# Graph network layer: VectorE instead of TensorE adds the gathered rows to z, and 26 instead of 28 quads are done by counts

## The reference

```python
h = jnp.maximum(_layernorm(x, axis=-1), 0.0)
e = jnp.concatenate([h[src], h[dst]], axis=1)          # 200000 x 128
m = jax.nn.relu(e @ W1 + b1) @ W2 + b2                 # W1 128x128, W2 128x64
s = jax.ops.segment_sum(m, dst, num_segments=12500)
cnt = jax.ops.segment_sum(ones, dst, num_segments=12500)
x = x + s / jnp.maximum(cnt, 1.0)[:, None]
```

## Time and profile before

| | us |
|---|---|
| runs | 2848.26, 2846.46, 2843.46; median 2846.46 |
| the profiled execution, whole | 2839.25 |
| its span | 2837.4 |
| TensorE matmul busy | 1548.3 (55%) |
| VectorE busy | 1428.9 (50%) |
| ScalarE busy | 1189.8 (42%) |
| GpSimd busy | 1372.7 (48%) |
| TensorE clock granted, mean | 0.749 of full |
| DMA, mean | 144 GB/s |

### The profile page before, as it was taken

How to read it: one execution, slowest core, us unless ns; L and a number is a source line. 1 busy time by engine, 2 the same in 40 slices (tenths; PEclk the granted TensorE clock), 3 DMA queues, 4 the chain that set the end, 5 groups by cost and what they waited for, 6 DMA issues and landing times.

```text
span 2837.4 us, 26976 instructions
## 1 busy us (share of the span) xinstructions
PE 1548.3 (55%) x8249; PEld 1183.2 (42%) x8250; DVE 1428.9 (50%) x3051; ACT 1189.8 (42%) x2414; POOL 1372.7 (48%) x1460
## 2 busy tenths in 40 slices
PE   1656565566465564455544555455455545555556
PEld 0545353444344443344433444344344434434444
DVE  3554343343324665456655666456565556655421
ACT  1223343444314544345444454344344444444444
POOL 6345545445555445444554435545544554554553
PEclk6878777788787777677776777767776777776778
DMA  4532222222134656556565566556565665665541
GB/s 90 163 109 60 59 61 59 60 59 58 58 98 144 202 181 189 167 169 200 179 192 154 178 188 200 186 159 183 184 192 168 186 191 174 183 186 157 174 119 43
DMA packets 258990, 408.46 MB, mean 144 GB/s; under 512 B 45128, under 2 KB 118749, under 8 KB 258841
## 3 DMA queue, kind: packets, MB, share of 16 engines
q1 hardware_dynamic: 211845, 312.84, 35.7%
q0 software_dynamic: 46432, 93.61, 12.5%
q10 hardware_dynamic: 564, 0.23, 0.0%
HBM read 388.12 MB, written 18.38 MB: 143 GB/s over the span
## 4 chain that ended last, share of the span: by engine, by line
PE 48%; issue 36%; another core or an unknown queue 9%; DVE 6%; ACT 1%; DMA 0%; DVEq 0%; SPq 0%; ACTq 0%
PE z L1374 16%; PE bank L1401 12%; PE z L1386 10%; DVE g L1153 4%; PE bank L1419 2%; PE bank L1408 2%; PE z L1445 2%; PE bank L1430 1%; PE z L1461 1%; DVE rows_b L936 1%; PE bank L1268 1%; DVE norms L920 1%; PE z L1268 1%; ACT g L812 0%
## 5 line engine op out<-in xcount | busy, mean ns | idle before, releaser
L672 POOL DMA_INDIRECT g<-p_table,src_e x1403 | 1326.1, 945 | 1425.3 <-PE bank L1401 960.5
L1153 DVE SCALAR_TENSOR_TENSOR g<-z,norms,g 128x1024 bf16<-128x1024 f32 (+1 forms) x884 | 1019.1, 1214 | 43.5 <-issue 25.3
L812 ACT ACTIVATE g<-z 128x1024 f32<-128x1024 f32 x182 | 185.6, 1020 | 1468.0 <-remote 1153.5
L1100 DVE TENSOR_TENSOR acc<-acc,bank 65x128 f32 x191 | 54.2, 284 | 1201.0 <-remote 1069.7
L1374 PE MATMUL z<-work 128*128 128x128 f32 x1464 | 258.8, 348 | 514.2 <-issue 482.9
L1374 PE MATMUL z<-w,work 128*128 128x128 f32 x1438 | 251.9, 345 | 484.3 <-issue 443.8
L1374 PEld LDWEIGHTS z<-work 128*128 128x128 f32 x1464 | 240.3, 256 | 546.0 <-issue 541.7
L1374 PEld LDWEIGHTS z<-w,work 128*128 128x128 f32 x1438 | 234.4, 253 | 512.3 <-issue 509.3
L1401 PE MATMUL bank<-work,g 128*128 128x128 f32 x2902 | 423.4, 307 | 15.4 <-issue 15.1
L1401 PEld LDWEIGHTS bank<-work,g 128*128 128x128 f32 x2902 | 414.1, 227 | 16.8 <-issue 16.7
L1386 PE MATMUL z<-g,ident 128*128 128x512 f32 x726 | 350.8, 605 | 5.8 <-issue 5.7
(11 more groups left out here) (161 smaller groups left out, 1063.6 us busy)
## 6 DMA issues: line engine op xcount, KB each, us to landing
g<-tally_table SPq DMA_DIRECT2D x816, 256.0 KB
rel_q<-rel_table SPq DMA_DIRECT2D x46, 512.0 KB
rows_b<-rel_table SPq DMA_DIRECT2D x45, 512.0 KB
g<-p_table,src_e POOLq DMA_INDIRECT x1403
g<-tally_table SPq DMA_DIRECT2D x68, 128.0 KB
work<-q_table SPq DMA_DIRECT2D x96, 64.0 KB
w<-q_table SPq DMA_DIRECT2D x96, 64.0 KB
g<-p_table SPq DMA_DIRECT2D x12, 512.0 KB
```

The costliest lines, as they stand in the source:

```text
L672: nc.gpsimd.indirect_dma_start(out=g[:, slot(n), j * HID:(j + 1) * HID], out_offset=None, in_=p_table, in_offset=bass.IndirectOffsetOnAxis ...
L812: nc.scalar.activation(rows_of_p(m), z[:, 0:HID * chunks_in(m)], ACT.Relu).then_inc(r_done, 1)
L1153: nc.vector.scalar_tensor_tensor(product[i % BUFFERS][:, 0:w], turned[:, 0:w], minus_q[:, d:d + 1], tally_row[i % BUFFERS][:, 0:w], ALU.ma ...
```

## The change

- `add_rows(m)` moves from TensorE to VectorE. One `tensor_tensor` adds z (PSUM) and the gathered rows (SBUF, `g`), and writes the sum over the gathered rows. It comes after the members and the tally rows of round m, and before `dense(m)` with its products.
- `relu` reads and writes these rows in `g`, no longer PSUM.
- `spread_q(m+1)` waits for VectorE's add of couple m (`z_done`) instead of the relu of couple m.
- TensorE's order becomes: `times_w2` of couple m-2, `sum_edges(m-1)`, `spread_q(m+1)`, `dense(m)`; so a couple's sum comes one round later. The waits that VectorE's own order now covers are dropped.
- 26 quads by counts: DENSE falls from 68 to 59, tallies from 236 to 212 (five a round, rounds 3 to 45, all low one-hot rows on ScalarE), products from 884 to 767 (rounds 52 to 176), and there are 183 couples.

```diff
-Q0 = 28
-GROUP_SIZES = ((128, 4), (320, 2), (QT * 128, 1))
+Q0 = 26
+GROUP_SIZES = ((126, 4), (320, 2), (QT * 128, 1))
-ROUND_TALLIES, TALLY_ROUND, TALLY_PLACES = 6, 3, 12
-VECTOR_TALLIES = (1, 4)
+ROUND_TALLIES, TALLY_ROUND, TALLY_PLACES = 5, 3, 10
-SPAN_ROUNDS = [10] * (SPANS - 1) + [6]
+SPAN_ROUNDS = [10] * (SPANS - 1) + [5]
...
             def relu(m):                                   # ScalarE
                 act.wait_ge(z_done, m + 1)
-                nc.scalar.activation(rows_of_p(m), z[:, 0:HID * chunks_in(m)], ACT.Relu).then_inc(r_done, 1)
+                nc.scalar.activation(rows_of_p(m), rows_of_p(m), ACT.Relu).then_inc(r_done, 1)
...
             def spread_of(m):                              # VectorE
-                if m >= 2:
-                    dve.wait_ge(zq_done, m - 1)
                 dve.wait_ge(rows_there[m // 2 % 2], 16 * (m // 4 + 1))
...
+            def add_rows(m):                               # VectorE
+                dve.wait_ge(zq_done, m + 1)
+                if 2 * m < RAW:
+                    dve.wait_ge(raw_p_done, 2 * m + 2)
+                else:
+                    dve.wait_ge(gathered[slot(Q0 + 2 * m) // 2], rows_landed(m))
+                nc.vector.tensor_tensor(rows_of_p(m), z[:, 0:HID * chunks_in(m)], rows_of_p(m), ALU.add)\
+                    .then_inc(z_done, 1)
...
-                if on_vector(p):
-                    nc.vector.tensor_scalar(low_hot[p % TALLY_PLACES], low_digits, low_key[:, j:j + 1], 0.0,
-                                            ALU.is_equal, ALU.add, accum_out=...)
...
                         for p in tallies(m):               # VectorE, round m
                             high_hot_of(p)
+                        add_rows(m)
                         dense(m)
...
             def spread_q(m):                               # TensorE
                 if m:
-                    pe.wait_ge(r_done, m)
+                    pe.wait_ge(z_done, m)
-                                                qw[i % WINDOWS], start=c == 0, stop=False)
+                                                qw[i % WINDOWS], start=True, stop=True)
-            def add_rows(m):
-                ...
-                    last = nc.tensor.matmul(z[:, 512 * (n % 2):512 * (n % 2) + w], ident[:, :], g[:, slot(n), 0:w],
-                                            start=False, stop=True)
...
-                for m in range(COUPLES):                   # TensorE
-                    add_rows(m)
-                    if m >= 2 and m - 2 == BLOCK_END[BLOCK[m - 2]]:
-                        times_w2(BLOCK[m - 2])
-                    dense(m)
-                    if m + 1 < COUPLES:
-                        spread_q(m + 1)
-                    sum_edges(m)
+                for m in range(COUPLES + 3):
+                    if m - 1 in (COUPLES - 2, COUPLES - 1):
+                        sum_edges(m - 1)
+                    if 2 <= m < COUPLES + 2 and m - 2 == BLOCK_END[BLOCK[m - 2]]:
+                        times_w2(BLOCK[m - 2])
+                    if 1 <= m < COUPLES - 1:
+                        sum_edges(m - 1)
+                    if m + 1 < COUPLES:
+                        spread_q(m + 1)
+                    dense(m)
```

More of the change, by code:

```diff
@@ L170 @@
 MEMBER_FROM = PRODUCT_ROUND
[L173 to L179, removed]
 def products_in(m):
@@ L304, in gnn_kernel @@
         low_hot = [above_ring(512 + 256 * k, 256, BF16) for k in range(TALLY_PLACES)]
-        high_hot = [above_ring(3584 + 64 * k, 64, BF16)[:, 0:125] for k in range(TALLY_PLACES)]
-        tally_stage = above_ring(4352, 256, U16)[0:125, :]
-        q_dense = above_ring(4352, 128, F32)[0:DENSE, :]
+        high_hot = [above_ring(3072 + 64 * k, 64, BF16)[:, 0:125] for k in range(TALLY_PLACES)]
+        tally_stage = above_ring(3712, 256, U16)[0:125, :]
+        q_dense = above_ring(3712, 128, F32)[0:DENSE, :]
         tally_row = [above_ring(512 * k, 512, U16) for k in range(BUFFERS)]
@@ L313, in gnn_kernel @@
         digit_i, digit, src_of_edge = (norms[:, NC * k:NC * (k + 1)] for k in range(3))
[L314 to L318, removed]
+        high_key, low_key = (norms[:, SPANS * DENSE + NC * k:SPANS * DENSE + NC * (k + 1)] for k in range(2))
+        added, by_count = (norms[:, SPANS * DENSE + DENSE * k:SPANS * DENSE + DENSE * (k + 1)] for k in range(2))
+        minus_q = norms[:, 1020:1020 + DENSE]
+        edges_d, of_node = norms[0:125, 1081:1081 + DGROUPS], norms[0:125, 1095:1095 + PER_GROUP]
+        assert 3 * NC <= SPANS * DENSE and SPANS * DENSE + 2 * NC <= 1020 and DENSE <= min(61, NC) and DGROUPS <= 14
         work = sb("work", [128, STAGES * UNIT_COLS + 512])
@@ L782, in spread_of @@
             def spread_of(m):
-                if m == SPREAD_FROM:
-                    act.wait_ge(spread_done, parts_to(m))
                 act.wait_ge(rows_there[m // 2 % 2], 16 * (m // 4 + 1))
@@ L846, in dense @@
                         stage_tallies(i)
-                of = [p for p in tallies(m) if not on_vector(p)]
+                of = tallies(m)
                 for p in of[0:1]:
                     far_low_of(p)
-                for p, after in zip(of, of[1:] + [None]):
-                    if after:
-                        far_low_of(after)
+                for p in of:
+                    if p + 1 in of:
+                        far_low_of(p + 1)
                     low_hot_of(p)
@@ L1126, in edge_keys_of @@
                     .then_inc(edge_keys, 1)
-                nc.vector.scalar_tensor_tensor(low_key, digit, -512.0, src_of_edge, ALU.mult, ALU.add)\
+                nc.vector.scalar_tensor_tensor(low_key, digit, 512.0, src_of_edge, ALU.mult, ALU.subtract)\
                     .then_inc(edge_keys, 1)
@@ L1137, in high_hot_of @@
                 if p == 0:
-                    dve.wait_ge(edge_keys, 10)
+                    dve.wait_ge(edge_keys, 5)
                 if p >= TALLY_PLACES:
@@ L1437, in tally @@
                 pe.wait_ge(high_hot_done, p + 1)
-                if not on_vector(p):
-                    pe.wait_ge(low_hot_done, on_scalar_to(p + 1))
+                pe.wait_ge(low_hot_done, p + 1)
                 if p == TALLY_FIRST[i]:
```

32 lines of the change are left out of this document (7 added, 25 removed).

## The result

| kernel | median, us | lowest to highest | ratio to before, 95% interval |
|---|---|---|---|
| before | 2844.96 | 2843.35 to 2848.26 | |
| changed | 2619.43 | 2612.39 to 2625.56 | 0.9205, 0.918 to 0.9231 |

The changed kernel takes 225 us less. The forecast was 2760 us: the time lies in its range, but the gain is 7.9% where 3.0% was forecast. The profiled execution took 2625.56 us, its span 2623.7.

A forecast was written before the change was run, and what follows sets the result against it. Bound: a loop of waits, 30.67 us for two couples, with TensorE's results withheld to the gather batch's end. 2839.25 - 86 - 14 + 14 = 2753, said as 2760 us; range 2610 to 2900, central forecast 2700 to 2820.

The forecast's parts named there:

- mix of hits and misses: Per gather batch: a hit has the next spread's result in time; a product-stretch miss, only at 22.8 us, loses about 2.0.
- A loop of waits bounds the kernel: GpSimd's batches: results of early matmuls reach others only at 22.8 us, making a loop of 30.67 us for two couples.
- TensorE's add worth nothing: In the loop: dropping TensorE's 1.88 us add a couple gains nothing by itself, since it stands behind the sum releasing GpSimd.
- The order "is what matters": TensorE: with the sum one round behind its spread, relu and spread leave the path behind the late results.
- Hit 28.4 us: Product stretch: only handover, copy, W2, sum and release follow the late result; 28.4 for 30.67, gaining 2.3 us.
- Four hits of five: Product stretch, 60 batches: 0.8 gain 2.3 us and 0.2 lose 2.0, together -86 us.
- rival 1: All product batches hit (-138) and three of four tally batches go at 23.1: 2656 us; chance 0.24 with beyond.
- Tally stretch -14 us: 19 batches at 29.3 us: half hits at 23.1, half misses at 34.0, mean 28.55, so -14 us.
- One couple more, +14: Whole kernel: the added couple costs half a loop, +14 us, its eight more gathers included.
- Sum: Whole kernel: 2839.25 - 86 - 14 + 14 = 2753 us, given as 2760 for a median.
- Clock: TensorE: fewer matmuls could keep its clock down, a batch's first 16 records taking 3.75 instead of 1.95 us; left unpriced separately.
- Rival 4: GpSimd's gathers lose VectorE's 1.22 us an add, +2.4 a batch, +220 over 91 batches: 3066 us; chance 0.03.

The follow-up runs named there:

- gatherless kernels: Kernel before and changed kernel, each with every gather after the first ring of places left out: 1781.4 and 1697.94 us.
- after_batch8: Changed kernel with GpSimd waiting for the sums before every couple (8 gathers), not every second (16): 2318.29 us, 0.8192 to before.
- add28_oldorder: Kernel before with the add on VectorE, TensorE's order as before and 28 quads by counts: 2526.44 us, 0.8925 to before.
- swap: Kernel before with only sum_edges(m) put ahead of spread_q(m + 1), add still on TensorE: 2672.21 us, 0.9448 to before.
- count26: Kernel before with 26 quads by counts alone, add still on TensorE: 2828.11 us, 0.9996 to before.
- before_batch8: Kernel before with GpSimd waiting for the sums before every couple (8 gathers), not every second: 2303.12 us, 0.8134 to before.
- old_batch8: Kernel before with the add on VectorE, TensorE's old order, 28 quads and batches of 8 gathers: 2301.66 us, 0.8134 to before.
- swap_batch8: Kernel before with the sum of couple m ahead of the spread of m+1 and batches of 8 gathers: 1841.41 us, 0.9956 to before.
- early_batch8: Kernel before with batches of 8 gathers and ScalarE's spread matrix made earlier from the product stretch on: 1842.6 us, 0.996 to before.

## Why the prediction was right or wrong

The mechanism was right, its sizes were not. The step that failed is the mix of hits and misses: one miss in five for the product stretch, -86 us, and half and half for the tally stretch, -14. The traces show no miss in 60 product batches, -174, and -68 in the tally stretch. A second step failed beside it, the order as the source of the gain.

- *A loop of waits bounds the kernel, through results withheld in a batch*: right with holds; the gatherless kernels and after_batch8 show it. But the prediction took it "as a rule of this kernel". It is a condition under which the kernel ran, and can be absent on the same chip.
- *TensorE's add worth nothing, VectorE's 1.22 off the path, relu +0.04*: 1.216, and 1.042 against 1.020; off the path in the batch shown. But that the move gives nothing without the new order failed: add28_oldorder keeps the order and gains 10.8%. There the add and its four wide matmuls are gone from what TensorE has queued when the hold begins. How much of the gain comes from that, how much from a relu that no longer waits for a TensorE result, and how much from a spread that waits for the add instead of the relu, the runs do not separate.
- *The order "is what matters"*: wrong as a ranking. It does matter alone (swap, 5.5%), but beside VectorE's add the old order is better by 2.6% with long batches (2526.44 against 2594.07) and 1.9% with short ones.
- *Hit 28.4 us*: measured 27.58 in the batch shown. The counts' turn (0.60) ran earlier in the batch, and the sum took 3.57 for 3.75.
- *Four hits of five*, so -86 us: this term was the most mis-sized. Product loops fell by 2.9 us on the mean where 1.44 was forecast: 60 x -2.9 = -174. All 60 are hits: no loop lies between 32.1 and 33.3, and 49 lie between 27.3 and 28.8. A spread that ends at 3.0 after the start passes, at the edge where I had put one in five outside. All hits at 2.3 would be rival 1's -138; most of the rest is the hit's own size, 27.7 for 28.4.
- *Tally stretch -14 us*: 20 x -3.4 = -68. Most loops are 24 to 25 or 28 us; 34.0 does not occur, and 23.1 only in the last two, from 780.8 on. The miss was mis-built. I put add, spread, tallies and sum in a row behind the late result; in the changed order the sum that frees GpSimd stands ahead of the spread and does not wait for the late add. In the batch at 319.2 the tallies start at 342.33 for 1.94, the sum at 344.06 for 2.97, and the next batch at 347.30: 28.1.
- *One couple more, +14*: not seen by itself with holds; half a loop is 13 to 14, but count26, which has that couple with the lighter products and tallies, took 1.1 us more than before. Without holds the changed kernel took 8.9 more.
- *Sum*: -174 - 68 + 14 = -228, against 213.7 between the spans. The 14 between are not explained: no run shows the +14 as it stands in the sum, and the loops of the two kernels do not end at the same couple.
- *Clock*: left inside the miss share. It stayed at 0.73 in the product stretch, and the 16 records behind the hold took 3.75 us before and 3.57 after, so no cost shows there. In the tally stretch it fell from 0.78 to 0.73, and without holds the mean over the execution was 0.83 for the changed kernel against 0.91. That is the way in which the rule of the Trainium skill that was weighed (TensorE: Matmul & The Clock Gate, "The HAM clock gate") points, that activity is what releases the throttle; no run shows that it cost time. The reading of the earlier trace rows was loose: 0.61, as a mix of full and half clock, puts about four fifths of 1452 to 1465 at the lower level, not half, which only strengthens what was read from it.
- *Rival 4*, VectorE slowing gathers: 948 ns against 945. It fell.

## What to carry to other kernels

When results reach their readers many microseconds after the records of the instructions that made them, look first at what the other engines' instruction streams do in that time, and cut that stream into shorter runs: two lines in GpSimd's wait gave 18.7%, the whole change 7.9%, and its best part, the add on VectorE in the old order, 10.8%. Count what stands between the late result and the wait that starts the next round. And compare a candidate with its base again in another session: both the base's bottleneck and the sign of the change may be those of a condition of the machine (0.92 and 1.006 here).

The best version depends on it. With holds, before_batch8 and old_batch8 (2303 and 2302 us) beat both kernels by far. Without, the fastest measured are two kernels that are level, both with TensorE's add and batches of 8: swap_batch8 (1841.41) and early_batch8 (1842.6), 0.4% better than before; GpSimd's count of gathers is the floor. The kernel before with batches of 8 alone was not run there.

## What the runs showed that I had not expected

- The same kernel on the same chip at 2827 us in one session and 1846 us in another; the changed kernel's gathers are recorded alike in both (948 and 946 ns, 1.25 us apart). What switches the condition, and by what path gathers hold TensorE, is open.
- With holds, most late updates of TensorE come at +22.7 from a batch's start (16 gathers) or +11.4 (8), and those in between at steps of 1.42 us or half of it. VectorE, ScalarE and SyncE work on in the same time until they need a result of TensorE: in the batch of the changed kernel shown VectorE runs a product every 1.2 us up to +13, ScalarE works up to +8.6, and SyncE issues six loads of counts between +7.3 and +13.7.
- A small pause after four gathers is enough: 5 iotas, 1.41 us, took the changed kernel from 2619 (in its own session) to 2418 us.
- A gather of 128 rows costs 1.25 us of GpSimd from one to the next, with half the bytes 1.25, with half the rows 1.20 (the last two measured without holds).
